# Making the next tile's first one-hots at the end of a tile, in the first layer of a graph network kernel

## What is computed

```python
def _L0_gnn_ref(node_feat, W_emb, b_emb, bases, w_coe, self_loop, ..., src, dst, etype):
    h = node_feat @ W_emb + b_emb
    norm = _edge_norm(etype, dst, h.dtype)
    for l in range(L):
        W = jnp.einsum('rb,bdf->rdf', w_coe[l], bases[l])
        T = jnp.einsum('nd,rdf->rnf', h, W)
        msg = T[etype, src] * norm
        agg = jax.ops.segment_sum(msg, dst, num_segments=N)
        h = agg + h @ self_loop[l]
        h = bn_gamma[l] * (h - bn_mean[l]) * jax.lax.rsqrt(bn_var[l] + BN_EPS) + bn_beta[l]
        h = jax.nn.relu(h)
    return h
...
edge_index = jnp.stack([src, dst])
x = _layernorm(x + _L0_gnn_ref(x, ..., src, dst, edge_type_8), axis=-1)
x = _layernorm(x + _L1_gnn_ref(x, src, dst), axis=-1)
x = _layernorm(x + _L2_gnn_ref(x, edge_index, ...), axis=-1)
x = _layernorm(x + _L3_gnn_ref(x, edge_attr_128, src, dst), axis=-1)
```

## Time and profile before

| | us |
|---|---|
| median of three runs | 6646.34 |
| lowest, highest | 6645.26, 6676.93 |
| the profiled execution | 6596.08 |
| its span, first to last instruction | 6594.3 |

### The profile page before, as it was taken

One profiled execution on the slowest core, in us unless ns is written; L12 is line 12 of the kernel. 1 busy time (PEld: TensorE's weight loads), 2 busy tenths in 40 slices (PEclk: granted clock), 3 DMA queues, 4 the chain that ended last, 5 costly groups with the idle time before them and its releaser, 6 DMA issues. The chain is left out here.

```text
span 6594.3 us, 158005 instructions
## 1 busy us (share of the span) xinstructions
PE 4572.3 (69%) x54120; PEld 3419.2 (52%) x54121; DVE 3830.4 (58%) x8449; ACT 2466.9 (37%) x3932; POOL 2432.9 (37%) x2046
## 2 busy tenths in 40 slices
PE   5465556556666666666666499999989566666879
PEld 2244444444444444444444366666655366666868
DVE  4155555555555555555555566666640699999942
ACT  2122323223323323323323366666620355555700
POOL 0444444444454444454444000000000077776700
PEclk9777777777777777787777699999999778888889
DMA  5444444444444444444444422222259333344378
GB/s 199 139 126 138 139 137 142 136 136 138 139 138 138 140 135 137 141 139 137 139 137 142 146 77 80 77 79 77 78 189 299 111 142 145 148 156 150 113 234 282
DMA packets 678649, 935.70 MB, mean 142 GB/s; under 512 B 150867, under 2 KB 573374, under 8 KB 672542
## 3 DMA queue, kind: packets, MB, share of 16 engines
q1 hardware_dynamic: 469222, 545.66, 26.1%
q10 hardware_dynamic: 152888, 273.31, 11.3%
q0 software_dynamic: 56448, 115.72, 7.0%
HBM read 653.23 MB, written 281.17 MB: 142 GB/s over the span
## 5 line engine op out<-in xcount | busy, mean ns | idle before, releaser
L643 POOL DMA_INDIRECT f_rows<-table,f_recs x1715 | 1654.0, 964 | 1902.3 <-DMA f_recs<-edge_records 1187.8
L756 PE MATMUL f_acc<-f_rows,f_hot 128*128 128x264 f32 x3430 | 1214.2, 521 | 366.7 <-issue 285.1
L756 PEld LDWEIGHTS f_acc<-f_rows,f_hot 128*128 128x128 f32 x3430 | 868.8, 263 | 573.2 <-issue 348.4
L2067 PE MATMUL a_psum<-state_and_spare,a_weights 128*128 (+1 forms) x4802 | 664.3, 309 | 303.6 <-DVE a_weights L2200 168.9
L2017 POOL TENSOR_TENSOR a_weights<-a_powers,a_counts 128x896 f32<-128x896 f16 x245 | 713.6, 2917 | 315.9 <-ACT a_powers L2107 285.6
L2067 PEld LDWEIGHTS a_psum<-state_and_spare,a_weights 128*128 128x128 f32 x4802 | 653.7, 225 | 317.2 <-issue 215.0
L1224 ACT ACTIVATE g_grow<-g_gps 128x512 f16<-128x512 f32 x1225 | 667.1, 595 | 343.1 <-PE g_gps L1161 343.1
L816 ACT ACTIVATE f_counts_by_destination<-f_pm 128x896 f16<-128x896 f16 x343 | 314.5, 917 | 1011.5 <-PE f_pm L723 836.3
L705 PE MATMUL f_cnt<-f_dhot,state_and_spare 32*128 32x32 f16 x9604 | 239.2, 182 | 614.2 <-issue 614.1
L1181 PE MATMUL g_zps<-g_ohot,g_grow 32*128 32x256 f16 x19992 | 655.7, 269 | 0.0
L1263 DVE TENSOR_SCALAR g_ohot<-count,slot_target 128x256 f16<-128x256 f16 x2499 | 537.2, 282 | 152.4 <-PE g_zps L1181 147.0
(11 more groups left out here) (280 smaller groups left out, 6006.6 us busy)
## 6 DMA issues: line engine op xcount, KB each, us to landing
f_rows<-in_edge_attr SPq DMA_DIRECT2D x343, 320.0 KB
g_srow<-slot_sources SPq DMA_DIRECT2D x245, 320.0 KB
counts_by_destination_f<-f_counts_by_destination ACTq DMA_DIRECT2D x343, 224.0 KB
no_edge_penalty<-f_pen ACTq DMA_DIRECT2D x343, 224.0 KB
s_ring<-counts_by_destination_f SPq DMA_DIRECT2D x98, 784.0 KB
a_pen<-no_edge_penalty SPq DMA_DIRECT2D x49, 1568.0 KB, 10.0
a_counts<-counts_by_source_f SPq DMA_DIRECT2D x49, 1568.0 KB, 6.8
e_ring<-counts_by_source_f SPq DMA_DIRECT2D x343, 224.0 KB, 3.7
```

What stands on the lines that cost most here:

```text
L643: e.indirect_dma_start(out=rows[:, j, 0:D], out_offset=None, in_=k.table_d[0], in_offset=bass.IndirectOffsetOnAxis(ap=recs[:, j, 4:5].bitc ...
L756: m = e.matmul(acc[:, 0:GW], hot[:, j, :], rows[:, j, :], start=j == 0, stop=j == SLOTS - 1)
L2067: m = e.matmul(psum[:, 4 + i // 3, i % 3 * (D + 4):i % 3 * (D + 4) + D + 1], weights[:, j, i * P:(i + 1) * P], k.msg[:, bass.ds(hb * SEG + ...
```

## The change

`tile_rows` and the one-hots of group 0 become functions of their own, `own_rows` and `one_hots`. At the end of every tile but the last, behind `rows_of_slots(t)`, VectorE now makes `own_rows(t + 1)` and `one_hots(t + 1, 0)`, and only then goes to `take(t)` and `hits(t + 1)` of the next tile. Group 0 is left out of the loop over groups, so `close` follows on `hits` directly. A drain is added behind `own_rows`. The last tile is written out behind the loop, since it has no next one. No other engine's program is changed.

```diff
--- before.py
+++ after.py
@@ -876,9 +876,22 @@
         def _(e):
             quads = lambda ap: ap.rearrange("p (u c) -> p u c", c=QCOLS)
 
+            def own_rows(t):
+
+                e.tensor_scalar(tile_rows, count_up[:, 0:P], k.tbase[:, bass.ds(t, 1)], None, ALU.subtract)
+                e.drain()
+
+            def one_hots(t, g):
+
+                e.wait_ge(rec_in[g], (t + 1) * 16)
+                e.wait_ge(ring, t * GROUPS + (g + 1))
+                s = slice(g * PER, (g + 1) * PER)
+                e.tensor_tensor(hot[:, s, :], repeat(tile_rows, PER), spread(recs[:, s, 0], P), ALU.is_equal)
+                e.tensor_tensor(rows[:, s, 2 * D:], repeat(k.iota8[:, :], PER),
+                                spread(recs[:, s, 3], RELATIONS), ALU.is_equal).then_inc(hot_made, 1)
+
             def hits(t):
 
-                e.tensor_scalar(tile_rows, count_up[:, 0:P], k.tbase[:, bass.ds(t, 1)], None, ALU.subtract)
                 e.wait_ge(wrec_in, (t + 1) * (16 * QUARTERS))
                 e.tensor_tensor(quads(inw[:, :]), quads(wrec[:, :, 5]),
                                 spread(k.window[:, bass.ds(t, 1), :].rearrange("p a u -> p (a u)"), QCOLS), ALU.is_equal)
@@ -1013,17 +1026,14 @@
             e.memset(key_t[:, :, :], 0.0).then_inc(blank, 1)
             e.memset(far[:, :], -FAR).then_inc(blank, 1)
             e.wait_ge(ring, GROUPS)
-            def tile(t, first):
+
+            def tile(t, first, final):
                 if not first:
                     take(t - 1)
                 hits(t)
                 for g in range(GROUPS):
-                    e.wait_ge(rec_in[g], (t + 1) * 16)
-                    e.wait_ge(ring, t * GROUPS + (g + 1))
-                    s = slice(g * PER, (g + 1) * PER)
-                    e.tensor_tensor(hot[:, s, :], repeat(tile_rows, PER), spread(recs[:, s, 0], P), ALU.is_equal)
-                    e.tensor_tensor(rows[:, s, 2 * D:], repeat(k.iota8[:, :], PER),
-                                    spread(recs[:, s, 3], RELATIONS), ALU.is_equal).then_inc(hot_made, 1)
+                    if g:
+                        one_hots(t, g)
                     if g == 0 and not first:
                         close(t - 1)
                     if 1 <= g <= QUARTERS:
@@ -1038,10 +1048,16 @@
                     if g == QUARTERS + 1:
                         columns(t)
                 rows_of_slots(t)
-
-            tile(0, True)
-            with e.Fori(1, NT) as t:
-                tile(t, False)
+                if not final:
+                    own_rows(t + 1)
+                    one_hots(t + 1, 0)
+
+            own_rows(0)
+            one_hots(0, 0)
+            tile(0, True, False)
+            with e.Fori(1, NT - 1) as t:
+                tile(t, False, False)
+            tile(NT - 1, False, True)
             take(NT - 1)
             close(NT - 1)
             keys(NT - 1)
```

## The result

The changed kernel takes **6556.18 us** (median of 4 runs, 6543.28 to 6567.91). The kernel before took 6661.64 us beside it (median of 4, 6645.26 to 6680.33). The ratio is **0.9841 [0.9808, 0.9873]**: faster by about 105 us. The forecast of 6646 us, no change, was wrong, and the range, whose low end was 6570, did not hold the time either. Two later comparisons, on two chips, gave 0.9843 [0.9768, 0.9919] and 0.984 [0.9789, 0.9891].

The account below looks back on a forecast made before the run. The prediction took the first phase to be bound by POOL's gathers starving TensorE and SP of instructions, with the turn of tiles hidden under run A. Terms 0 + 0 + 0 left the median at 6646 us, no change (chance 0.47); range 6570 to 6720.

Parts of the forecast that it names:

- TensorE starves under POOL's gathers, and so does SP: First phase: while POOL gathers, other engines get instructions only in a trickle; L705's gaps without a seen wait total 614.1 us.
- The turn: Passage between tiles at `take`: group 0 starts 4.18 us sooner, 200.6 us over 48 turns if all counted; forecast 0.
- run A: First of POOL's three runs of gathers in the usual tile: 10 gathers, 12.3 us; `place` gets through only behind it.
- B: Second of POOL's three runs of gathers in the usual tile: 15 gathers, 18.6 us, forecast to start as before.
- the zero of the turn: At `place` and SP's `wrec` loads: both still wait behind run A, so the earlier group 0 is worth 0 us.
- the slack of 0.7 us: Group 2's gathers, last five of run B: due at 2044.1, could start at 2043.4 despite a late clock.
- The clock's price: TensorE waking at 1.2 GHz after a longer rest delays keys and group 2: 0 to 1 us per turn, taken as 0.
- the second rival: A part counts: earlier arrival at `place` makes pauses before group 2's gathers more frequent; 60 us faster, 6586 us, chance 0.11.
- `close` 1.3 us sooner ... neither is waited for: 0: Behind `take`: `wrec_used` comes 0.3 us and `close` 1.3 us sooner, but nothing waits for either, so 0.
- The third rival: Short tiles vanish: group 2's records land sooner, run B stays whole; 62 us slower, 6708 us; chance 0.28 with late clock wake.
- the first rival: The turn counts in full: run A does not hold `place`, each tile shortens by 4.18 us; 6445 us, chance 0.14.

Follow-up runs that it names:

- held to 3.9 us: Changed kernel, TensorE's group 0 waiting until `hits` has made its cells, 3.9 us behind `take`: 0.9845 where chips starve, 0.9932 (5610.37 us) where not.
- The order alone: Changed kernel, TensorE's group 0 held to 5.0 us behind `take`, where it started before, leaving only VectorE's new order: 0.9934.
- group 0 at 6.9 us: Changed kernel, TensorE's group 0 held until `close` has made the new state, 6.9 us behind `take`: 1.0022.
- the change with a forced pause: Changed kernel, POOL's gathers of group 2 also waiting for TensorE's first block of counts: 0.9659 (5452.62 us) where nothing starved, 0.9675 where starved.
- the pause alone: Kernel before, POOL's gathers of group 2 also waiting for TensorE's first block of counts: 0.9712 and 0.9715, both where chips starve.
- the kernel with late `wrec` loads: Kernel before, SP's four `wrec` loads moved behind those of group 3: 5655.72 us, against 5646.35 for before, where nothing starved.
- paced: Kernel before, POOL waiting after every group of five gathers until they have landed: 0.9541 where starved; 6277.21 us, 11% slower, where not.

## Why the prediction was wrong

- **TensorE starves under POOL's gathers, and so does SP: right**, where the chip is in that condition. Without gathers the gaps are 0.0. That it is the supply of instructions which runs out is a reading: the rows show slow issue that no wait explains, and not its reason.
- **The turn is moved under run A and counts nothing there: right.** 255.3 us of idleness left the sums and 254.8 us came at `place`. B starts 7.5 us behind A, as before. Holding group 0 at 3.9 instead of 0.6 us loses nothing.
- **The step that failed is the zero of the turn, "So B starts as before. Worth: 0 us", and the slack of 0.7 us with it.** B does start as before, but the sum also took it to stay one run of 15 gathers. It comes apart before group 2 in 31, 31 and 28 of 47 tiles (before 7 and 11), and those tiles are 4.4 to 5.0 us shorter than the others of the same traces. The slack paragraph looked at the right place and left out SP: it lets SP's load follow TensorE's group 2 at once. In the tiles with a pause the load came 4.9 to 5.5 us behind it at the median of the three traces. I had myself found SP held under run A, and had not asked the same of it under B.
- **The clock's price, "between 0 and 1 us per turn, at most 48 us", had its sign open to one side only.** The late wake came (nine matmuls in 2.05 us instead of 1.15), and the choice of 0 held in the median tile: group 2 gained back by its own shorter time what it lost (27.4 and 27.8 against 27.6 us). Where a late group 2 does delay its gathers, I gave this the sign of a loss, though I had written that a run of 15 gathers holds TensorE until 2.6 us behind its end, so that a run which breaks after 10 frees it some 6 us sooner; the second rival even describes that pause. Adding 1.4 us of useless work gave 0.9953. The wake alone is not the gain, though: held to 3.9 us, half of the pauses come without it.
- **The second rival, "a part counts", was the one that came**, at 0.11. Its size was low: I took one more pause in eight turns at 10 us each, 60 us; it was 21 more in 47 tiles at 5 us each, 105 us.
- **"`close` 1.3 us sooner ... neither is waited for: 0" failed too.** The order alone gives 0.9934 [0.9903, 0.9965], some 40 us. This rests on one comparison, and its way through the tile is not found.
- **The third rival, "the short tiles vanish", fell.** The trace after has 6 tiles under 65 us, like before. It decides at group 2, as I said, but group 2 did not come earlier. It shows where a change towards it does go: group 0 at 6.9 us, 5 pauses, 1.002.
- **"`place` going through under A" (the first rival) fell** where the chip starves. In the other condition the change with a forced pause took 51.3 (from the kernel with late `wrec` loads, level with before there) - 47.2 = 4.1 us off a tile, near the 4.18 us of the full turn; but the pause alone did not run there, nor the bare change, so that is a hint and no more. The Trainium skill's page "Runtime: NRT & Kernel Launch", section "Instruction fetch mechanics", which has the supply of instructions as mostly hidden, was at odds with the trace again (482.4 us of gaps after) and agrees with the other condition (4.4 us).
- **The range** was too narrow by 14 us. It leaned on the traced execution's mixture of tiles as the usual one. The traces outside the first phase agree (6596.08 - 3369.9 = 3226 us before, 3223 us in the third run of the changed kernel), so an execution of 6661.64 us has a first phase of about 3436 us, an estimate: 71.6 us a tile, no short ones to speak of. More of the gain was open than the trace of before showed.

Still open: why SP gets late to group 2's records in some tiles and not in others, and so why the change makes these tiles more frequent; why the first 1.1 us of the earlier start make 12 pauses more (15 to 27), and whether they do; how much of the gain goes through the cold wake and how much through `close`. That pauses before group 2 make the time shorter is shown by forcing them. That the change gains by them rests on the counts, on the tiles within each trace, and on the two not adding up.

## What to carry to other kernels

Where an engine's supply of instructions runs dry under another's work, cost a change also by where it leaves that work's pauses, not only by delays along a chain: a wait or even wasted work that puts a pause where the starved engine needs one can gain more than it costs, and a second pause may gain nothing. Look at all tiles before one tile's story is believed: the tile shown above has a late TensorE, which most tiles with a pause do not have. When a mechanism is found with a slack of under a microsecond, both signs of crossing it have to be priced. And a change that only moves idle time (255 us from one line to another) can still move the time by an effect two groups later.

## What the runs showed of the hardware

The kernel before took 6570 to 6629 us in 13 runs on one chip, 5642 to 5652 us in seven runs on it 24 minutes later, and 6659 to 6707 us in nine runs another 42 minutes later; on other chips 6621 to 6713 us. In the condition of the seven runs only 1.4 to 4.4 us of gaps stood at the tiny matmuls of the four kernels traced there (the kernel before is not one of them). Gathers took the same 0.97 us in both. I found nothing in the profile that says what differs. The starving itself is worth 960 us of 6600, nine times the change. This is what it looks like on TensorE under POOL's gathers, in the tile shown above: one to three tiny matmuls about every 0.7 us, and nothing that is waited for.

```profile
2114.10 0.23 PE L705 MATMUL f_cnt<-f_dhot,state_and_spare 32*128 32x32 f16 x3 [1.23 <-issue]
2114.84 0.19 PE L705 MATMUL f_cnt<-f_dhot,state_and_spare 32*128 32x32 f16 x1 [0.51 <-issue]
2115.57 0.21 PE L705 MATMUL f_cnt<-f_dhot,state_and_spare 32*128 32x32 f16 x2 [0.54 <-issue]
2116.28 0.18 PE L705 MATMUL f_cnt<-f_dhot,state_and_spare 32*128 32x32 f16 x1 [0.50 <-issue]
```

So what a change is worth can differ between the conditions, even in sign (paced: 0.954 and 1.11). The changed kernel alone was not run where nothing starves; held to 3.9 us it gave 0.9932 there.
